# Layer 1's FiLM with tokens on partitions, its rows through DRAM and its result turned by DMA

## The reference

```python
# layer 0: linear attention with 8 heads of 32
xn = ln(x) * w + b
q  = softmax(xn @ Wq + bq)            # over the features of a head
k  = softmax(xn @ Wk + bk + mask)     # over the tokens
v  = (xn @ Wv + bv) * mask
y  = q @ (k.T @ v)                    # per head
# layer 1: softmax attention with 16 heads of 16, same names
y  = softmax(q @ k.T + mask) @ v
# both layers end with FiLM, SiLU and a projection
scale, shift = split(silu(cond) @ W_emb + b_emb)      # one row of 256 each per item
h  = (ln(y) * w2 + b2) * (1 + scale) + shift
x  = x + silu(h) @ W_out + b_out
```

## Time and profile before

| | |
|---|---|
| runs | 822.73, 827.06, 825.99 us; median 825.99 us |
| profiled execution, its own time | 826.59 us |
| its span, first to last instruction | 824.9 us |
| instructions | 27262 |
| TensorE matmul busy | 797.7 us, 97% of the span |
| TensorE weight load busy | 572.0 us, 69% |
| VectorE busy | 735.6 us, 89% |
| ScalarE busy | 704.5 us, 85% |
| GpSimd busy | 688.7 us, 83% |
| DMA queue q1 | 84.36 MB, 42.4% of 16 engines |
| mean granted TensorE clock | 0.989 of full |

### The profile page before, as it was taken

One profiled execution on the slowest core, in us unless ns is written; L12 is line 12 of the kernel. 1 busy time (PEld: TensorE's weight loads), 2 busy tenths in 40 slices (PEclk: granted clock), 3 DMA queues, 4 the chain that ended last, 5 costly groups with the idle time before them and its releaser, 6 DMA issues.

```text
span 824.9 us, 27262 instructions
## 1 busy us (share of the span) xinstructions
PE 797.7 (97%) x9407; PEld 572.0 (69%) x9407; DVE 735.6 (89%) x1488; ACT 704.5 (85%) x1658; POOL 688.7 (83%) x1021
## 2 busy tenths in 40 slices
PE   7998999999999999999999999999999999999995
PEld 3575776777777777677777777777777777666643
DVE  6899999998989999989898889989898989898962
ACT  2366678999898998898898998889989999999995
POOL 8579899999878999789898999888889987896423
PEclk9899999999999999999999999999999999999998
DMA  7522355354344443334545543353454433444411
GB/s 184 153 40 67 96 140 133 81 119 112 86 108 109 105 126 102 98 90 98 122 107 136 121 98 84 84 134 106 110 122 109 109 88 80 99 104 128 116 34 39
DMA packets 149276, 86.11 MB, mean 104 GB/s; under 512 B 87404, under 2 KB 141802, under 8 KB 149130
## 3 DMA queue, kind: packets, MB, share of 16 engines
q1 hardware_dynamic: 149140, 84.36, 42.4%
HBM read 39.64 MB, written 25.80 MB: 79 GB/s over the span
## 4 chain that ended last, share of the span: by engine, by line
PE 41%; issue 12%; POOL 9%; DVE 9%; DMA 2%; SPq 1%; ACT 1%; POOLq 0%; DVEq 0%; ACTq 0%
PE banks L708 11%; PE banks L861 7%; PE banks L716 5%; PE banks L835 4%; PE banks L848 4%; PE banks L723 3%; DVE NM L1308 3%; PE banks L738 2%; PE banks L787 2%; PE banks L871 2%; DVE st L1199 1%; POOL YN L2015 1%; POOL rs L2011 1%; POOL ZHL L2036 1%; POOL SH L2088 1%
## 5 line engine op out<-in xcount | busy, mean ns | idle before, releaser
L1308 DVE TENSOR_REDUCE NM<-banks 128x4 f32<-128x1024 f32 x256 | 306.4, 1212 | 25.1 <-PE banks L835 24.0
L1807 ACT ACTIVATE wraw<-banks 128x1024 f32<-128x1024 f32 x154 | 155.9, 1034 | 8.0 <-PE banks L848 7.3
L2011 POOL TENSOR_TENSOR rs<-ve,nhalf 128x2 f32<-128x2 f32 x128 | 89.7, 703 | 31.6 <-ACT ve L1682 31.4
L1807 ACT ACTIVATE PX<-banks 128x1024 f32<-128x1024 f32 x102 | 103.5, 1035 | 8.6 <-PE banks L848 7.3
L2088 POOL TENSOR_TENSOR SH<-ST,SH 128x512 f16<-128x512 f32 x64 | 74.4, 1164 | 31.4 <-ACT SH L1771 31.4
L708 PE MATMUL banks<-wo,SH 128*128 128x256 f16 x768 | 94.9, 274 | 4.5 <-POOL SH L2088 4.4
L708 PE MATMUL banks<-wv,ZT 128*128 128x256 f16 x768 | 93.5, 273 | 1.4 <-DVE wv L1404 0.5
L835 PE MATMUL banks<-SK,SQ 51*128 51x256 f16 x1024 | 92.5, 272 | 0.8 <-ACT wemb L1815 0.3
L848 PE MATMUL banks<-SQ,SK 53*128 53x256 f16 x1024 | 90.6, 271 | 2.1 <-DVE NM L1308 1.0
L2036 POOL TENSOR_TENSOR ZHL<-Z,ZHL 128x256 f16<-128x256 f32 x128 | 87.5, 704 | 2.6
L861 PE MATMUL banks<-wraw,V 128*32 128x256 f32 x1232 | 87.2, 385 | 0.8 <-DVE NM L1308 0.8
(11 more groups left out here) (186 smaller groups left out, 1879.5 us busy)
## 6 DMA issues: line engine op xcount, KB each, us to landing
scr<-AB SPq DMA_DIRECT2D x64, 256.0 KB, 2.6
X<-in_x_dram SPq DMA_DIRECT2D x32, 256.0 KB, 2.8
SK<-scr SPq DMA_DIRECT2D x64, 128.0 KB, 2.9
SQ<-scr SPq DMA_DIRECT2D x64, 128.0 KB, 2.7
out_dram<-wemb SPq DMA_DIRECT2D x32, 256.0 KB, 2.5
SK<-scr SPq DMA_DIRECT2D x64, 64.0 KB, 2.9
SQ<-scr SPq DMA_DIRECT2D x64, 64.0 KB, 2.7
wemb<-in_L_cond_W_emb_dram SPq DMA_DIRECT2D x1, 1024.0 KB, 5.5
```

The lines of the kernel that those rows point to most:

```text
L1308: V.tensor_reduce(NMe[:, c, :, 2 * g:2 * g + 2], banks[:, n:n + 2, :].rearrange("p a (h m) -> p a h m", m=T), AX.X, ALU.max, negate=True). ...
L1807: A.activation(px(v % 5), banks[:, n:n + 2, :].rearrange("p a n -> p (a n)"), ACT.Exp, scale=r_uu).then_inc(S["exp"])
L2011: G.tensor_tensor(rs[:, b % 2, l, :], ve[:, b % 2, l, :], nhalf[:, :], ALU.pow).then_inc(S[f"r{l}"])
```

## The change

Layer 0 keeps its FiLM as it was. In layer 1 the FiLM is done with tokens on partitions.

- Scale and shift of all items are computed once as rows (`film_token`), scaled, and written to DRAM (`fmd`). For each item SP loads its row of 512 floats to all 128 partitions (`fr1`, into the single buffer `FR`).
- `yn1` writes into `HH`, GpSimd multiplies it by the scale row (`fa1`) and adds the shift row (`fb1`), and ScalarE makes one tanh of 128x512 from it with a scale in a register. `ST` is formed as before; `sh1` and `sl1` write the two parts to `SHL`, and SP turns them by a DMA transpose (`sT1`) into `SHT`, which o1 reads. The transposes `y1T` and layer 1's four bank reads are gone. `FR`, `SHL` and `SHT` have one buffer each.
- The mean is subtracted as it stands in `mv`; ScalarE no longer copies it negated, and `moments` waits for the reader of the item before instead of for ScalarE.
- The high parts h0 and h1 are made by ScalarE, each one instruction of 128x512 instead of two of 128x256 on GpSimd. `vm` moves from GpSimd to ScalarE.
- The orders of all five engines, `BANK` and `FREED` are written anew. In the setup, both layers' weight scales stand before the first projection, and GpSimd clears `V1` before it makes the constants.

```diff
+            def film_in(b, l, i):
+                e.wait_ge(S[f"fb{l}"], b)
+                if b == 0:
+                    e.wait_ge(l_fm[l], 16)
+                e.dma_start(FR[:, i].rearrange("p a n -> p (a n)"), fmd[l, b].unsqueeze(0).to_broadcast([P, 2 * D])).then_inc(d_fr[l][b % 2], 16)
+
+            def turn_out(b, l, i):
+                e.wait_ge(S[f"sl{l}"], b + 1)
+                e.wait_ge(S[f"o{l}"], b)
+                e.dma_start(SHT[:, i].rearrange("p j k (t n) -> p (j k t) n", t=2),
+                            SHL[:, i].rearrange("p j k t n -> p (j k t n)"), transpose=True).then_inc(d_s[l][b % 2], 16)
...
-            def y1T(b):
-                e.wait_ge(S["yn1"], b + 1)
-                clear(e, "gy1T", b)
-                transposes(home("gy1T", b), YN[:, 1]).then_inc(S["y1T"])
-
             def o1(b):
-                e.wait_ge(S["sl1"], b + 1)
+                e.wait_ge(d_s[1][b % 2], 16 * (b // 2 + 1))
                 clear(e, "go1", b)
...
-                tok_major(bank(home("go1", b)), SH[:, 1], W["o", 1]).then_inc(S["o1"])
+                tok_major(bank(home("go1", b)), SHT[:, 0], W["o", 1]).then_inc(S["o1"])
...
             def moments(b, l):
                 e.wait_ge(S[f"s{l}"], b + 1)
-                e.wait_ge(S[f"n{l}"], up(b - 1))
+                e.wait_ge(S[("c0", "yn0", "c1", "yn1")[l]], up(b - 1))
...
-                A.activation(nm[:, b % 2, l, :], mv[:, b % 2, l, :, 0], ACT.Copy, scale=-1.0)
...
             def th1(b):
-                th_of(b, 1)
+                if b == 0:
+                    e.wait_ge(l_rt[1], 1)
+                e.wait_ge(S["fb1"], b + 1)
+                e.wait_ge(S["st1"], b)
+                A.activation(TH[:, 1], HH[:, 1], ACT.Tanh, scale=r_t[1]).then_inc(S["th1"])
 
             def sh1(b):
-                sh_of(b, 1)
+                e.wait_ge(S["st1"], b + 1)
+                if b >= 1:
+                    e.wait_ge(d_s[1][(b - 1) % 2], 16 * ((b - 1) // 2 + 1))
+                A.activation(SHL[:, 0, 0].rearrange("p k t n -> p t k n"),
+                             ST[:, 1].rearrange("p t (k n) -> p t k n", k=2), ACT.Identity).then_inc(S["sh1"])
...
+            def h0(b):
+                e.wait_ge(S["c0"], b + 1)
+                if b >= 2:
+                    e.wait_ge(d_z[0][b % 2], 16 * (b // 2))
+                A.activation(ZHL[:, 0, b % 2, 0].rearrange("p k t n -> p t k n"),
+                             Z[:, 0].rearrange("p t (k n) -> p t k n", k=2), ACT.Identity).then_inc(S["h0"])
...
+            def vm(b):
...
+                    i = A.activation(V1[:, r, c, :, 0:16], V1t[:, c, :].rearrange("p (h f) -> p h f", f=16), ACT.Copy,
+                                     scale=mcol[:, 1, c, b:b + 1])
+                i.then_inc(S["vm"])
...
             def apply(b, l, dst, src, s):
                 for t in range(2):
-                    i = G.tensor_scalar(dst[:, t, :], src[:, t, :], nm[:, b % 2, l, t:t + 1], rs[:, b % 2, l, t:t + 1], ALU.add, ALU.mult)
+                    i = G.tensor_scalar(dst[:, t, :], src[:, t, :], mv[:, b % 2, l, t, 0:1], rs[:, b % 2, l, t:t + 1],
+                                        ALU.subtract, ALU.mult)
                 i.then_inc(S[s])
...
             def yn1(b):
                 e.wait_ge(S["r3"], b + 1)
-                e.wait_ge(S["y1T"], b)
-                apply(b, 3, YN[:, 1], Y[:, 1], "yn1")
+                e.wait_ge(S["st1"], b)
+                apply(b, 3, HH[:, 1], Y[:, 1], "yn1")
+
+            def fa1(b):
+                e.wait_ge(S["yn1"], b + 1)
+                e.wait_ge(d_fr[1][b % 2], 16 * (b // 2 + 1))
+                G.tensor_tensor(HH[:, 1], HH[:, 1], both(FR[:, 0, 0, :]), ALU.mult).then_inc(S["fa1"])
+
+            def fb1(b):
+                e.wait_ge(S["fa1"], b + 1)
+                G.tensor_tensor(HH[:, 1], HH[:, 1], both(FR[:, 0, 1, :]), ALU.add).then_inc(S["fb1"])
 
             def sl1(b):
-                sl_of(b, 1)
+                e.wait_ge(S["sh1"], b + 1)
+                for k in range(2):
+                    i = G.tensor_tensor(SHL[:, 0, 1, k], ST[:, 1].rearrange("p t (k n) -> p t k n", k=2)[:, :, k, :],
+                                        SHL[:, 0, 0, k], ALU.subtract)
+                i.then_inc(S["sl1"])
```

More of the change, by code:

```diff
@@ L92 @@
+    "gty1": "22244657772075624637106574413706",
+    "go1": "52346734736635536070501242313777",
 }
@@ L277 @@
     "yn0 y0T th0 st0 sh0 sl0 o0 x1 s2 a2 n2 r2 c1 h1 z1 xb1 q1p qa spq k1p ka spk v1p vt vm rows max nh np cols "
-    "exp pv yt ty rd Y1 s3 a3 n3 r3 yn1 y1T th1 st1 sh1 sl1 o1 o").split()
+    "exp pv yt ty rd Y1 s3 a3 n3 r3 yn1 fa1 fb1 th1 st1 sh1 sl1 o1 o").split()
 def up(n):
@@ new lines, in _ @@
+            z0(9); spq(4); r2(5); yn0(6); qs(8); c1(5); z1(5); sl1(0); kn(9); r0(10); c0(10); sl0(6); r1(7); z0(10)
+            r3(1); yn1(1); nh(3); fa1(1); xb1(4); fb1(1); spq(5); yn0(7); xb0(8); qs(9); spk(5); r2(6); c1(6)
+            sl1(1); z1(6); kn(10); r0(11); c0(11); r1(8); sl0(7); yn0(8); z0(11); r3(2); nh(4); yn1(2); xb1(5)
+            fa1(2); spk(6); fb1(2); xb0(9); spq(6); r2(7); c1(7); qs(10); z1(7); sl1(2); kn(11); r0(12); c0(12)
+            sl0(8); r1(9); yn0(9); r3(3); yn1(3); fa1(3); nh(5); fb1(3); xb1(6); spk(7); xb0(10); z0(12); r2(8)
@@ new lines, in _ @@
+            spk(10); qs(14); z1(11); r0(16); c0(16); kn(15); sl1(6); z0(16); r3(7); yn1(7); nh(9); sl0(12); spk(11)
+            xb1(10); r1(13); fa1(7); xb0(14); fb1(7); yn0(13); r2(12); c1(12); spq(11); z1(12); qs(15); sl1(7)
+            kn(16); sl0(13); r0(17); r1(14); c0(17); yn0(14); r3(8); z0(17); nh(10); yn1(8); xb1(11); fa1(8)
+            xb0(15); spq(12); fb1(8); spk(12); r2(13); c1(13); qs(16); r0(18); z1(13); c0(18); sl1(8); kn(17)
+            r1(15); z0(18); sl0(14); yn0(15); r3(9); yn1(9); nh(11); fa1(9); xb1(12); fb1(9); qs(17); xb0(16)
@@ new lines, in _ @@
+            spk(13); r2(14); c1(14); spq(13); z1(14); r0(19); c0(19); sl1(9); kn(18); sl0(15); r3(10); z0(19)
+            r1(16); nh(12); yn1(10); xb1(13); fa1(10); fb1(10); xb0(17); yn0(16); spk(14); r2(15); c1(15); spq(14)
+            z1(15); sl1(10); r0(20); qs(18); c0(20); kn(19); z0(20); sl0(16); r1(17); nh(13); r3(11); yn0(17)
+            yn1(11); xb1(14); fa1(11); xb0(18); spk(15); fb1(11); spq(15); qs(19); r2(16); r0(21); c1(16); sl1(11)
+            kn(20); z1(16); c0(21); r1(18); yn0(18); z0(21); sl0(17); r3(12); nh(14); yn1(12); qs(20); xb1(15)
@@ new lines, in _ @@
+            z0(27); qs(26); nh(20); r3(18); xb1(21); yn1(18); spk(22); spq(22); xb0(25); fa1(18); fb1(18); r2(23)
+            c1(23); sl1(18); z1(23); kn(27); r0(28); c0(28); z0(28); r1(25); yn0(25); sl0(24); nh(21); r3(19)
+            xb1(22); spk(23); yn1(19); xb0(26); fa1(19); fb1(19); r2(24); spq(23); c1(24); qs(27); z1(24); kn(28)
+            sl1(19); r1(26); r0(29); c0(29); yn0(26); z0(29); qs(28); sl0(25); nh(22); xb1(23); r3(20); spk(24)
+            xb0(27); yn1(20); spq(24); fa1(20); fb1(20); r2(25); c1(25); z1(25); kn(29); r1(27); sl1(20); r0(30)
@@ L2241 @@
+            fb1(29); sl1(29); r3(30); yn1(30); fa1(30); fb1(30); sl1(30); r3(31); yn1(31); fa1(31); fb1(31)
+            sl1(31); xb1(31)
 _L0 = ['ln_w', 'ln_b', 'Wq', 'bq', 'Wk', 'bk', 'Wv', 'bv', 'W_emb', 'b_emb', 'ln2_w', 'ln2_b', 'W_out', 'b_out']
```

1183 lines of the change are left out of this document (595 added, 588 removed), and 195 rows, old and new, of the table FREED.

## The result

The changed kernel takes 973.99 us (median of 4 runs, 972.41 to 976.48) against 826.52 for the kernel before: ratio 1.1795, 95% interval 1.1745 to 1.1845. I had forecast 819.5 in a range of 807 to 834, and none of my rivals went past 845. The change costs 147 us.

The account below looks back on a forecast made before the run. The prediction took TensorE to bound the kernel, busy 23.6 of 23.8 us an item. From 826.6 us, -9.2 (TensorE), -2 (ScalarE at the end) and +4.4 (drain) gave 819.8, stated as 819.5, range 807 to 834.

Parts of the forecast that it names:

- Part 3: GpSimd's work per item: operations moved out and in sum to +0.2 us, giving 21.2 us an item.
- Part 1: TensorE loses the four transposes of y1T per item: 15.4 us of work in all, bounds 14.1 and 18.9.
- What TensorE's 15.4 us become: Share of TensorE's saving kept in the loop: 0.6, its share of the chain, so -9.2 us, bounds 0 and -15.4.
- Part 2: ScalarE's work per item: copies and layer 1 reads out, tanh, h0, h1 and vm in; +0.6 us, to 22.2.
- Rival (b): ScalarE or VectorE becomes the bound and the item stays as long: 824 to 829 us; chance 0.22 together with (d).
- (d): Rival: the change doesn't do what it says, the row landing late for fa1; chance 0.22 together with Rival (b).
- Part 4: SP's queue and DMA: two more 256 KB transfers an item, hidden at share 0.53; 0 us, bounds 0 and +5.
- Part 5: The drain after the last Y1: 18.5 us instead of 14.15, so +4.4 us, bounds +3.5 to +6.3.
- Part 6: ScalarE at the end: -2 us, bounds 0 and -4; the head: 0, with 3 us both ways.
- Rival (c): Slower: GpSimd's XB1 waits for O through the four XB1 buffers; about 838 us, from 831 to 845; chance 0.18.

Follow-up runs that it names:

- e1_negmean: The changed kernel with ScalarE again copying the mean negated and GpSimd adding it instead of subtracting: 847.01 us, ratio 1.0255 against the kernel before.
- g3_one_transpose: The kernel before with one transpose of layer 1's result per item instead of four, that quarter read for all four: 823.45 us, ratio 0.9973.
- g1_row_once_no_turn: e1_negmean with the scale and shift row loaded for item 0 only and o1 reading SHL unturned, without the turn: 831.43 us, ratio 1.0074.
- h3_before_transposes: The kernel before with each of the four transposes of layer 1's result made twice: 835.87 us, ratio 1.0141.
- g2_transposes_back: e1_negmean with four idle fp32 transposes per item ahead of o1's products, in o1's own bank: 854.82 us, ratio 1.0380 against the kernel before.
- g4_row_small: e1_negmean with the row loaded to 16 partitions instead of 128 from item 1 on, all issues and waits kept: 837.79 us, ratio 1.0157.
- e5_forms: The changed kernel with four forms of GpSimd's TENSOR_SCALAR side by side: subtract first, subtract second, no subtract, both subtract: 942.97 us in a single run.
- e2_before_sub: The kernel before with GpSimd subtracting the mean as it stands in mv, without ScalarE's negated copy, and moments waiting for its reader: 955.31 us, ratio 1.1576.

## Why the prediction was wrong, step by step

**Part 3, GpSimd, failed, and with it everything.** I wrote "out" and "in" for the operations that move and gave the subtraction of the mean no term at all: it kept its place, its tile and its shape, and I took its duration to be that of the addition (0.56 to 0.59 us). The kernel before had no TENSOR_SCALAR with a subtract on GpSimd, so it needed bounds from both sides, like the other operations that I had no row for. The measured term is +5.4 us an item, +127 us in all (e1_negmean), which puts GpSimd at 26.5 us an item. The other terms that I set out for GpSimd held: fa1 and fb1 1.27 and 1.28 us, and without the subtract, in e1_negmean, its work from 200 to 700 us is 439.12 us for 166 maxes or 20.75 items, 21.2 us each. The Trainium skill (GPSIMD Engine Reference, Engine selection) calls GpSimd's one-input work roughly line rate. No run here measures whether the addition's 0.56 us is that; the subtract's 1.23 us is 2.2 times as long on the same tile, so it holds for one of the two at most.

**Part 1 and "What TensorE's 15.4 us become": the work was sized right, its worth wrong.** I gave TensorE's saved work a price of 0.6, for its share of the chain, with a busy share of 98% behind it. g3_one_transpose gives 2.3 of 11.0 us, 0.2, and g1_row_once_no_turn, with the change's whole saving and both transfers gone, has a middle only 2.6 us shorter than before. So about -3 us stands where I put -9.2. What the new orders and the new bank table do to it by themselves no run separates. Work added has another price: h3_before_transposes costs 11 us for 14.4 (0.76), and in the changed order g2_transposes_back 7.8 (0.54). I read this as a kernel that stands where TensorE and the rest end about together; an average over the chain is neither slope. The view by stretches shows why the busy share doesn't tell; from 200 to 700 us, beside the line of the kernel before, in g3_one_transpose and in h3_before_transposes:

```profile
200.00:700.00 500.00, 494.21 (x6123) 362.85 (x6112) 456.48 (x886) 455.42 (x1080) 442.08 (x649) 1.00 0.44 107
```

```profile
200.00:700.00 500.00, 496.49 (x6078) 372.81 (x6072) 449.12 (x874) 448.89 (x1060) 434.17 (x638) 1.00 0.45 105
```

TensorE is 99% busy in all three, with four of these transposes an item before, one and eight. A matmul has a duration of 273 ns and its successor starts about 0.11 us behind it (twelve of them in 1.47 us), so an idle time shorter than the difference, 0.16 us by this estimate, lies under the bars. That this is where g3_one_transpose's saving went I infer from the share that stayed; no view here shows those gaps.

**Part 2, ScalarE, held.** 457.85/20.75 = 22.1 us an item in e1_negmean (22.2 forecast); tanh 0.63, h0 and h1 0.63, vm 0.52 where I took 0.42. Rival (b), to which I had given 0.22 with (d), is close to what came of the TensorE gain, but its mechanism is argued and not shown. With the transfers out, g1_row_once_no_turn has VectorE at 470 and ScalarE at 468 of 500 us, where they were 455 and 454, and VectorE's maxima wait for TensorE 10.5 us instead of 19.7; but TensorE is still 98% busy there.

**Part 4, the DMA, was the second error.** I read the share right (0.53 forecast, 0.56 measured) and wrote "hidden too in the mean", with 5 us as the upper bound from a single place in the chain. The two transfers cost 15.6 us. I looked for lateness only in what is queued behind them and gave o1's wait for its own turned result a term in the drain alone; that it is read, and not the load by itself, is worth 8.1 us of the middle beside the row. Landing became later for all, by 0.1 to 0.5 us: X 3.3 us in e1_negmean against 2.8 before, the row itself 3.9. My picture of what is queued on SP was not it for the row; g4_row_small keeps every issue and wait of it. Why both together cost more than their sum is not settled. In the kernel before they do so with neither read (10.7 us against 2.3 and 2.9), which may lie with the DMA engines or with SP, since SP has one issue and one wait more at each step as well; in the changed order they do so only when the turn is read.

**Part 5, the drain, held.** 18.5 us forecast (of its steps, O of item 30 was summed to 7.1 us where the terms give 7.0); in e1_negmean the last Y1 ends at 828.27 and the span at 847.9, 19.6 us later. From its timeline, the last item:

```profile
827.85 0.42 DVE L1365 TENSOR_TENSOR Y<-banks,rd 128x256 f32<-128x256 f32 x1
...
836.99 1.29 POOL L2231 TENSOR_TENSOR SHL<-ST,SHL 128x256 f16<-128x256 f32 x2 [2.55 <-ACT SHL L1895]
...
838.31 1.23 SPq L549 DMA_TRANSPOSE SHT<-SHL  x1
841.39 2.26 PEld L758 LDWEIGHTS banks<-wo,SHT 128*128 128x128 f16 x12 [7.02 <-DMA SHT<-SHL]
841.40 2.74 PE L758 MATMUL banks<-wo,SHT 128*128 128x256 f16 x12 [6.54 <-DMA SHT<-SHL]
```

The turn takes 3.1 us from issue to the first matmul, as the landing times of the kernel before said. My estimate from the bandwidth in the Trainium skill (DMA: Bandwidth & Descriptors, Latency and other measured facts) was 1.0 us; the runs show three times that for a single transfer of this size. Most of the remaining difference is o1, 2.74 us against 1.86, behind a wait of 6.5 us; the profile page shows a granted clock of 0.6 of full in the last slice, against 0.8 in the kernel before.

**Part 6.** The head cost 2.3 us (first max at 95.1 against 92.8) where I put 0 with 3 both ways. From the last max to the last Y1 I had -2 us for ScalarE; it is 1.6 longer (21.4 and 23.0). So the 23.0 us between the spans of e1_negmean and the kernel before divide into head +2.3, middle +13.6, the stretch up to the last Y1 +1.6 and drain +5.5; and the middle, by g1_row_once_no_turn, into +16.2 for the transfers and -2.6 for all the rest. My sum had 0, -9.2, -2 and +4.4 for the four. (These give 819.8 us on the profiled execution and 819.2 on the median; I wrote 819.5.)

**Rival (c)** was not it: XB1's wait for O is 4.4 us over the whole span of the changed kernel and 7.7 in e1_negmean, less than the 11.4 before. No version with the whole of the change's work beats the kernel before; g3_one_transpose is 0.3% below it and leaves out three quarters of FiLM's input.

## What to carry to other kernels

An edit that swaps one ALU operation for another on the same tile is a new instruction until a row shows it: price it from both sides, or measure it alone, before any sum of stages. In this loop, where all four engines are nearly full, taking work from the fullest was worth a fifth of it and adding to it a half to three quarters. Two small transfers that are each nearly hidden need not be hidden together: price them together, with the wait of whoever reads them, and not by the mean share.

## What the runs showed of the hardware

- A GpSimd TENSOR_SCALAR of 128x256 fp32 takes 0.56 us with add and mult and 1.23 us as soon as one of its two operations is a subtract, in either place (e5_forms; e2_before_sub in the other kernel). A GpSimd TENSOR_TENSOR with a subtract shows nothing like it (AB, with fp16 out, 1.17 us for 128x512, against 1.29 for XB's addition of the same size, with fp32 out).
- In the changed kernel, where TensorE has more idle time (425 us busy of 500 against 495), its granted clock is lower as well, in every stretch above: 0.96 from 200 to 700 us against 1.00; e1_negmean has 1.00 again.
- A transfer turned by DMA, 256 KB, lands in 3.1 to 3.7 us (medians of the kernels here, the highest in h4_before_both); the last one at the end of e1_negmean takes 3.0 to 3.1, no less than in the full loop.
